# Summing squares over the features: four transposes and a DVE reduction in place of products with a column of ones

## The chip, the cores and the metric

One core of a Trainium2 chip runs the whole program. The metric is device time in microseconds (us) of that core. PE is TensorE (matrix products and transposes), DVE is VectorE, ACT is ScalarE, POOL is GpSimd, SP issues DMAs. PSUM is the memory that TensorE writes into, in banks of 512 fp32 numbers for each of 128 partitions; SBUF is the working memory.

## The reference, cut to what matters

The input x is 16 sequences of 512 tokens with 256 features. For each sequence (a chunk, below):

```python
xn = _layernorm(x, axis=-1)
# branch s, on xn
x1 = causal_dwconv(rmsnorm(xn, conv_norm_g), ...) + xn
x2 = min_gru(rmsnorm(x1, gru_norm_g), gru_w) + x1
s  = gelu(rmsnorm(x2, ff_norm_g) @ w1.T + b1) @ w2.T + b2 + x2
# branch g, on xn
g  = silu(fp4_linear(silu(fp4_linear(xn, w_gate)) * fp4_linear(xn, w_up), w_down))
out = x + s * g
```

with `rmsnorm(x, gamma) = x / max(sqrt(sum(x * x)), 1e-12) * 16 * (gamma + 1)`, the sum over the 256 features. The change is in the second and third rmsnorm, on `x1` and on `x2`. The first is worked out from the layernorm's variance and isn't touched. `fp4_linear` rounds both operands to 4-bit values in blocks of 16; the recurrence of the GRU is a scan along the 512 tokens.

## The kernel before, in words

All weights stay in SBUF. Products of fp32 data are made from two fp32r parts, `_hi` (a copy that ScalarE casts) and `_lo` (what DVE subtracts), as three fp32r products each (`product`, L881). In the s branch the features lie on the partitions and the tokens in the free dimension: `x1`, `xs` and others are 128 x 2 x 512, two blocks `k` of 128 features. DVE adds the two blocks of squares (`add_squares`, L503) into `sqs`, 128 x 512. What is left is the sum over 128 partitions.

Each engine runs its own list of instructions in the written order, and semaphores hold it where it needs another's result. A chunk is `body(c, ...)` on each engine, 16 times: the first without the tail of a chunk before it, the last without the front of one behind it, the 14 between all alike. There the work of three chunks is interleaved by hand: the g branch of chunk c (`gate_up`, `hidden`), the rest of the s and g branches of c - 1 (`hq_transposes`, `down`, `ff2`), and the layernorm, first norm, fp4 rounding and convolution of c + 1 (`front_...`).

A norm goes through these steps, twice in a chunk:

1. ScalarE squares both blocks; DVE `add_squares` (L503).
2. TensorE `sum_squares` (L928): for each of the four tiles of 128 tokens a product of `sqs` with a column of ones, which gives a column of 128 sums, tokens on the partitions.
3. DVE `clamp_sums` (L508) scales by 1/256 and clamps, 128 x 4, into `ss_row`.
4. GpSimd `rms_scale` (L346) raises to the power -1/2, into `inv_rms`.
5. TensorE `spread_scale` (L937) puts the scale of each token on all partitions, by four transposes of a broadcast column.
6. DVE `scaled` (L516) multiplies, ScalarE makes `xs_hi` (L750), DVE `scaled_low` (L522) makes `xs_lo`, and TensorE goes on with `gru` or `ff1`.

For the first norm of a chunk (on `x1`, before `gru`) the sums and the spread scale go to banks 0 and 1 of `w_ps`; for the second (on `x2`, before `ff1`) to two banks of `gu_ps`. On TensorE `gate_up(c, 1, ...)` stands before the first sum and `down(c - 1, 1)` and `gate_up(c, 2, ...)` between it and its spread; `ff2(c - 1, 1)` stands before the second sum and `down(c - 1, 3)` between it and its spread; then `ff2(c - 1, 3)`, `ff2(c - 1, 2)` (L993 is each one's first two transposes) and `ff1`. On DVE the order around the first clamp is

```python
                hidden(c, 1)
                if tail:
                    ratios = fp4_ratios(hid[:, 2, :], NBI, scales)
                ...
                clamp_sums(c * 2, w_ps[:, 0, :])
                if tail:
                    hidden_values(c - 1, 2, fp4_round(NBI, ratios))
                    gelus_low(c - 1, range(5, KF))
                hidden(c, 2)
```

where `hidden` (L475) waits for both products of `gate_up`, and `gelus_low` (L491) makes three low parts. Around the second it is `output(c - 1, 0)` (L549), `clamp_sums`, `front_rows(c + 1)` (L444, the layernorm's rows `xn`, which ScalarE's `xc` at L698 waits for), the scales of the next fp4 rounding, and `scaled`.

Of the kernel before, what the change touches and what calls it, by code (L numbers as in the profile page):

```python
# [23 lines left out]
ALU = mybir.AluOpType  # L24
ACT = mybir.ActivationFunctionType
AX = mybir.AxisListType

P = 128
LN_EPS = 1e-5
NORM_FLOOR_SQ = 1e-24  # L30
# [29 lines left out]
def mixed_recurrent_kernel(nc, x, columns, pw_t, gru_t, w1_t, w2_t, w_gate, w_up, w_down, identity, out):  # L60
    B, L, D = x.shape
    T = L // P
    KD = D // P
# [12 lines left out]
    with ctx:  # L76
        def sb(name, shape, dt=F32):
            return ctx.enter_context(nc.sbuf_tensor(name, shape, dt))
# [10 lines left out]
        def sem(name):  # L89
            return ctx.enter_context(nc.semaphore(name))  # L90


        ident = sb("ident", [P, P])
        ones = sb("ones", [P, P])
        neg_half = sb("neg_half", [P, T])
        carrier = sb("carrier", [P, 1])
        cols = sb("cols", [P, KD * 9 + KF])
# [29 lines left out]
        xq_lo = sb("xq_lo", [P, KD, L], F32R)  # L127

        x1 = sb("x1", [P, KD, L])
        ss_row = sb("ss_row", [P, T])  # L130
        inv_rms = sb("inv_rms", [P, T])
        xs = sb("xs", [P, KD, L])
        sq = xs
        sqs = xs[:, 0, :]
# [104 lines left out]
        dve_step = sem("dve_step")  # L239
# [37 lines left out]
        def over_chunks(engine, body):  # L277

            body(0, 0, False, True)
            for c in range(1, B - 1):  # L280
                body(c, c % 2, True, True)
            return body(B - 1, 1, True, False)


        @block.sync
        def _(sp):
            sp.dma_start(x_in[:], x_v[0]).then_inc(ld_x, 16)
            sp.dma_start(gu_rows[:, 0:NFULL, :],
                         w_gate[0:NFULL * P, :].rearrange("(t p) d -> p t d", p=P)).then_inc(ld_gu, 16)
            sp.dma_start(gu_rows[:, NFULL:2 * NFULL, :],  # L290
                         w_up[0:NFULL * P, :].rearrange("(t p) d -> p t d", p=P)).then_inc(ld_gu, 16)
            sp.dma_start(gu_rows[0:LAST, WT - 1, :], w_gate[NFULL * P:NI, :]).then_inc(ld_gu, 16)
            sp.dma_start(gu_rows[LAST:P, WT - 1, :], w_up[NFULL * P:NI, :]).then_inc(ld_gu, 16)
            sp.dma_start(dn_rows, w_down.rearrange("(t p) n -> p t n", p=P)).then_inc(ld_dn, 16)
            sp.dma_start(w1_f, w1_t.rearrange("(t p) n -> p t n", p=P)).then_inc(ld_w1, 16)
            sp.dma_start(w2_f.rearrange("p a (k n) -> p (a k) n", n=D), w2_t.rearrange("(t p) n -> p t n", p=P)).then_inc(ld_w2, 16)

            def load(c):

                sp.wait_ge(xn_ready, c)  # L300
                sp.dma_start(x_in[:], x_v[c]).then_inc(ld_x, 16)

            def store(c):
                sp.wait_ge(out_ready, c + 1)
                sp.dma_start(out_v[c], o[:]).then_inc(stored, 16)
                sp.dma_start(x_res[:], x_v[c + 1]).then_inc(xres_ready, 16)

            sp.dma_start(x_res[:], x_v[0]).then_inc(xres_ready, 16)
            load(1)
            load(2)  # L310
            with sp.Fori(0, B - 3) as i:
                store(i)
                load(i + 3)
            store(B - 3)
            store(B - 2)
            for t in range(T):
                sp.wait_ge(last_ready, t + 1)
                sp.dma_start(out_v[B - 1][:, t, :], o[:, t, :]).then_inc(stored, 16)
            sp.wait_ge(stored, 16 * (B - 1 + T) + 16)


        @block.gpsimd
        def _(pool):
            steps = Steps(pool_step)
            nc.gpsimd.memset(ones[:], 1.0)
            constants = steps.mark(nc.gpsimd.memset(neg_half[:], -0.5))
            nc.gpsimd.memset(hq[:, :, NI:KI * P], 0.0).then_inc(constants_ready, 1)
            pool.wait_ge(pool_step, constants)

            def layernorm_scales(c, base):  # L330

                steps.start(base)
                pool.wait_ge(stats_ready, c + 1)
                TT = nc.gpsimd.tensor_tensor
                TT(rstd[:], ln_in[:], neg_half[:], ALU.pow).then_inc(rstd_ready, 1)
                pool.wait_ge(rstd_ready, c + 1)
                n = steps.mark(TT(rms_t[:, 1, :], rms_t[:, 0, :], rstd[:], ALU.mult))
                pool.wait_ge(pool_step, n)
                n = steps.mark(TT(rms_t[:, 2, :], rms_t[:, 1, :], rstd[:], ALU.mult))
                pool.wait_ge(pool_step, n)  # L340
                TT(rms0[:], rms_t[:, 2, :], neg_half[:], ALU.pow).then_inc(rms0_ready, 1)

            def rms_scale(n):

                pool.wait_ge(ss_ready, n + 1)
                nc.gpsimd.tensor_tensor(inv_rms[:], ss_row[:], neg_half[:], ALU.pow).then_inc(inv_ready, 1)  # L346

            def output_sum(c, parity):

                pool.wait_ge(sg_ready, T * (c + 1))  # L350
                pool.wait_ge(xres_ready, 16 * (c + 1))
                nc.gpsimd.tensor_tensor(o[:], o[:], x_res[:], ALU.add).then_inc(out_ready, 1)

            layernorm_scales(0, 1)
            for j, (_, src, hi, lo) in enumerate(split_weights):
                for k in range(KD):
                    pool.wait_ge(whi_ready, KD * j + k + 1)
                    nc.gpsimd.tensor_tensor(lo[:, k, :], src[:, k, :], hi[:, k, :].bitcast(F32),
                                            ALU.subtract).then_inc(wlo_ready, 1)

            def body(c, parity, tail, front):
                rms_scale(c * 2)
                if front:
                    layernorm_scales(c + 1, 1 + (c + 1) * 2)
                rms_scale(c * 2 + 1)
                if tail:
                    output_sum(c - 1, 1 - parity)

            over_chunks(pool, body)
# [3 lines left out]
        def _(dve):  # L373
            V = nc.vector
            steps = Steps(dve_step)
# [129 lines left out]
            def clamp_sums(n, bank):  # L505

                dve.wait_ge(ss_done, n + 1)
                V.tensor_scalar(ss_row[:], bank[:, 0:T], 1.0 / D, NORM_FLOOR_SQ / D, ALU.mult,  # L508
                                ALU.max).then_inc(ss_ready, 1)

            def scaled(n, src, bank, ready):
# [26 lines left out]
            def weight_low(p):  # L538
                dve.wait_ge(wqhi_ready, p + 1)
                for (lo, src), (hi, _) in zip(weight_places(p, gu_lo), weight_places(p, gu_hi)):  # L540
                    last = V.tensor_tensor(lo, src, hi.bitcast(F32), ALU.subtract)  # L541
                last.then_inc(wqlo_ready, 1)
# [11 lines left out]
            s = steps.mark(V.tensor_scalar(gains[:], gains[:], 1.0, None, ALU.add))  # L554
            dve.wait_ge(dve_step, s)
            for k in range(KD):
                last = V.tensor_scalar(dww[:, k, :], dww[:, k, :], gains[:, 0, k:k + 1], None, ALU.mult)
# [32 lines left out]

            prologue_steps = steps.n
            quant = 6
            chunk_steps = 4 * quant + 2 * KD + (2 + quant) + KD
            first_steps = chunk_steps - 2

            def body(c, parity, tail, front):
# [15 lines left out]
                else:  # L612
                    down_weight(0)
# [3 lines that stand above are left out]
# [68 lines left out]
        def _(act):  # L685
# [112 lines left out]
            for j, (load, src, _, _) in enumerate(split_weights):  # L798
                act.wait_ge(load, 16)
                if j == 2:  # L800
                    break
                for k in range(KD):
                    A.activation(src[:, k, :], src[:, k, :], ACT.Copy,
                                 scale=gains[:, 1 + j, k:k + 1]).then_inc(wscaled, 1)
            for j, (_, src, hi, _) in enumerate(split_weights):
                for k in range(KD):
                    if j < 2:
                        act.wait_ge(wscaled, KD * j + k + 1)
                    A.copy(hi[:, k, :], src[:, k, :]).then_inc(whi_ready, 1)
# [61 lines left out]
        def _(pe):  # L871
            M = nc.tensor
# [50 lines left out]
            def sum_squares(n, bank, free):  # L923

                pe.wait_ge(sqs_ready, n + 1)
                pe.wait_ge(*free)
                for t in range(T):
                    last = M.matmul(bank[:, t:t + 1], sqs[:, t * P:(t + 1) * P], ones[:, 0:1],  # L928
                                    start=True, stop=True)
                last.then_inc(ss_done, 1)  # L930

            def spread_scale(n, bank, free):
# [74 lines left out]
            for p in range(NFULL + 1):  # L1007
# [4 lines left out]
                for k in range(KD):  # L1012
                    for t in range(tiles):
                        at = (2 * k + t) * P
                        last = M.transpose(w_ps[:, 2 + p % 2, at:at + P],
                                           hq[:, p % 2, t * D + k * P:t * D + (k + 1) * P], ident[:])
# [118 lines left out]
```

## Time and profile before

| | |
|---|---|
| median of 3 runs | 1121.58 us (1121.17 to 1121.89) |
| profiled execution, its own time | 1123.78 us |
| its span, first to last instruction | 1121.9 us |
| mean granted TensorE clock | 0.974 of full |
| busy: PE, PE weight loads, DVE, ACT, POOL | 1057.3, 961.4, 932.6, 603.7, 147.8 us |
| instructions on PE, on DVE | 6818, 1702 |

Times of instructions are from the profiled execution, in us from the start of its span. Matmuls are pipelined, so the busy times of neighbours overlap: how long a group of them holds TensorE is read from the distance between the start of its first and the start of what follows. "Idle before" is the time in which the engine had nothing to run, with the instruction that ended the wait.

### The profile page before, as it was taken

To read this page: it belongs to the slowest core of one execution; us is meant where nothing else is said; L and a number is where in the kernel's file an instruction comes from. 1 tells how busy PE (TensorE), PEld (TensorE's weight loads), DVE (VectorE), ACT (ScalarE), POOL (GpSimd) and SP (SyncE) were. 2 spreads that over 40 slices of the span, in tenths; PEclk is the share of its full clock that TensorE was granted. 3 is DMA by queue.
4 is the path that set the end of the run, shared out by engine and by line. 5 is a ranking of instruction groups with operands and counts; after the bars stand their busy time and mean duration, and the time that the engine had idled before them with its cause. 6 is when DMAs were issued, how large, how long until landed. Compare 5 with 4: busy or idle time off the path is not lost.

```text
span 1121.9 us, 17994 instructions
## 1 busy us (share of the span) xinstructions
PE 1057.3 (94%) x6818; PEld 961.4 (86%) x6818; DVE 932.6 (83%) x1702; ACT 603.7 (54%) x953; POOL 147.8 (13%) x124
## 2 busy tenths in 40 slices
PE   3276999999999999999999999999999999999987
PEld 2174898989989898999989899998989899898977
DVE  5957788998979889888988888888889989798855
ACT  4134556474655737465564746456564746557451
POOL 3101010110201011020202011020101102010010
PEclk9586999999999999999999999999999999999999
DMA  7000001010110101010010101001010100101010
GB/s 239 0 1 19 1 1 57 1 57 1 25 34 1 57 1 58 1 57 1 1 57 1 57 1 58 1 1 57 1 57 1 57 1 23 36 1 39 1 38 20
DMA packets 29364, 31.43 MB, mean 28 GB/s; under 512 B 1120, under 2 KB 28512, under 8 KB 29280
## 3 DMA queue, kind: packets, MB, share of 16 engines
q1 hardware_dynamic: 28448, 29.43, 8.5%
q8 instruction: 55, 0.90, 0.3%
q10 hardware_dynamic: 832, 0.87, 0.2%
q14 instruction: 29, 0.24, 0.1%
HBM read 21.90 MB, written 8.39 MB: 27 GB/s over the span
## 4 chain that ended last, share of the span: by engine, by line
PE 91%; DVE 6%; ACT 2%; issue 1%; DMA 0%; POOL 0%; ACTq 0%; DVEq 0%; POOLq 0%
PE gu_ps L881 46%; PE w_ps L881 32%; PE w_ps L945 4%; PE gu_ps L928 1%; PE w_ps L888 1%; PE w_ps L993 1%; PE w_ps L899 1%; PE gu_ps L888 1%; PE w_ps L928 1%; DVE q_y L398 1%; DVE q_amax L386 1%; PE w_ps L937 1%; PE gu_ps L937 1%; DVE hq L412 1%; DVE q_e L406 0%
## 5 line engine op out<-in xcount | busy, mean ns | idle before, releaser
L881 PE MATMUL gu_ps<-gu_hi,xq_hi 128*128 128x352 f32 x512 | 169.1, 330 | 1.0 <-DVE gu_lo L541 1.0
L881 PE MATMUL gu_ps<-gu_lo,xq_hi 128*128 128x352 f32 x512 | 166.9, 326 | 0.0
L881 PE MATMUL gu_ps<-gu_hi,xq_lo 128*128 128x352 f32 x512 | 166.6, 325 | 0.0
L881 PE MATMUL w_ps<-w_hi,act_hi 128*128 128x256 f32 x480 | 139.6, 291 | 0.0
L881 PE MATMUL w_ps<-w_hi,act_lo 128*128 128x256 f32 x480 | 134.6, 280 | 0.0
L881 PE MATMUL w_ps<-w_lo,act_hi 128*128 128x256 f32 x480 | 134.6, 280 | 0.0
L475 DVE TENSOR_TENSOR hid<-sl,gu_ps 128x704 f32<-128x704 f32 x64 | 56.8, 887 | 83.3 <-PE gu_ps L881 82.8
L881 PE MATMUL w_ps<-dn_hi,hqt_hi 128*128 128x256 f32 x384 | 116.5, 304 | 0.0
L768 ACT ACTIVATE g<-w_ps 128x256 f32<-128x256 f32 x64 | 24.6, 385 | 170.0 <-PE w_ps L881 169.9
L346 POOL TENSOR_TENSOR inv_rms<-ss_row,neg_half 128x4 f32<-128x4 f32 x32 | 40.7, 1270 | 550.2 <-DVE ss_row L508 550.2
L881 PE MATMUL w_ps<-dn_lo,hqt_hi 128*128 128x256 f32 x384 | 108.1, 281 | 0.0
L881 PE MATMUL w_ps<-dn_hi,hqt_lo 128*128 128x256 f32 x384 | 108.1, 281 | 0.0
L881 PE MATMUL gu_ps<-xs_hi,w_hi 128*128 128x512 f32 x256 | 103.6, 405 | 3.1 <-DVE xs_lo L522 3.1
L881 PE MATMUL gu_ps<-xs_hi,w_lo 128*128 128x512 f32 x256 | 102.1, 399 | 0.0
L881 PE MATMUL gu_ps<-xs_lo,w_hi 128*128 128x512 f32 x256 | 101.6, 397 | 0.0
L881 PEld LDWEIGHTS gu_ps<-gu_hi,xq_hi 128*128 128x128 f32 x512 | 97.3, 190 | 1.4 <-DVE gu_lo L541 1.4
L881 PEld LDWEIGHTS gu_ps<-gu_lo,xq_hi 128*128 128x128 f32 x512 | 97.4, 190 | 0.0
L881 PEld LDWEIGHTS gu_ps<-gu_hi,xq_lo 128*128 128x128 f32 x512 | 97.0, 189 | 0.0
L791 ACT ACTIVATE act<-gu_ps,cols 128x512 f32<-128x512 f32 x128 | 86.2, 687 | 15.2 <-PE gu_ps L881 14.8
L881 PEld LDWEIGHTS w_ps<-w_lo,act_hi 128*128 128x128 f32 x480 | 90.6, 189 | 0.0
L881 PEld LDWEIGHTS w_ps<-w_hi,act_hi 128*128 128x128 f32 x480 | 90.5, 188 | 0.0
L881 PEld LDWEIGHTS w_ps<-w_hi,act_lo 128*128 128x128 f32 x480 | 90.4, 188 | 0.0
(127 smaller groups left out, 2635.2 us busy)
## 6 DMA issues: line engine op xcount, KB each, us to landing
x_in<-x_dram SPq DMA_DIRECT2D x16, 512.0 KB, 5.9
x_res<-x_dram SPq DMA_DIRECT2D x16, 512.0 KB, 5.2
out_dram<-o SPq DMA_DIRECT2D x15, 512.0 KB, 3.4
act<-w_t_dram SPq DMA_DIRECT2D x1, 1024.0 KB, 11.8
w_f<-w_t_dram SPq DMA_DIRECT2D x1, 1024.0 KB, 14.3
act<-w_down_dram SPq DMA_DIRECT2D x1, 704.0 KB, 9.8
hid<-w_gate_dram SPq DMA_DIRECT2D x1, 640.0 KB, 6.3
hid<-w_up_dram SPq DMA_DIRECT2D x1, 640.0 KB, 9.3
```

What stands on the lines that cost most here:

```text
L346: nc.gpsimd.tensor_tensor(inv_rms[:], ss_row[:], neg_half[:], ALU.pow).then_inc(inv_ready, 1)
L386: s = steps.mark(V.tensor_reduce(am, blocks(src, nb), AX.X, ALU.max, apply_absolute_value=True))
L398: return steps.mark(V.scalar_tensor_tensor(blocks(q_y[:, 0:nb * FP4_BLOCK], nb), blocks(src, nb), UNIT, spread(q_inv[:, 0:nb], nb), ALU.mu ...
L412: return V.scalar_tensor_tensor(blocks(dst, nb), blocks(q_m[:, 0:nb * FP4_BLOCK].bitcast(BF16), nb), 1.0 / UNIT, spread(q_scale[:, 0:nb], ...
L475: V.tensor_tensor(hid[:, t, :].rearrange("p (h n) -> p h n", h=2), sl[:], gu_ps[:, 1, :, 0:HALF], ALU.mult).then_inc(hid_ready, 1)
L768: A.activation(g[:, t, :], bank[:, 0:D], ACT.Silu).then_inc(g_ready, 1)
L791: A.activation(act1[:, j, :], ff1_bank(j), ACT.Gelu, bias=b1c[:, j:j + 1]).then_inc(gelu_ready, 1)
L881: done = M.matmul(psum, l, r, start=first and i == 0, stop=last and i == len(terms) - 1)
L888: last = M.transpose(bank[:, t * P:(t + 1) * P], src[:, t, k * P:(k + 1) * P], ident[:])
L928: last = M.matmul(bank[:, t:t + 1], sqs[:, t * P:(t + 1) * P], ones[:, 0:1], start=True, stop=True)
L937: last = M.transpose(bank[:, t * P:(t + 1) * P], inv_rms[:, t:t + 1].to_broadcast([P, P]), ident[:])
L945: last = M.transpose(w_ps[:, 2 + k // 4, k % 4 * P:(k % 4 + 1) * P], hq[:, t % 2, k * P:(k + 1) * P], ident[:])
```

## The change

The product with a column of ones becomes a transpose of each 128 x 128 tile of `sqs`, four to a sum, into a whole bank of 128 x 512. Tokens are then on the partitions and the 128 features in the free dimension, and DVE sums those with a TENSOR_REDUCE from PSUM into `ss_sum`, 128 x 4. The clamp reads `ss_sum` after a wait for it. `ones` and its memset go.

```diff
-        ones = sb("ones", [P, P])
...
+        ss_sum = sb("ss_sum", [P, T])
...
-            nc.gpsimd.memset(ones[:], 1.0)
...
                 dve.wait_ge(ss_done, n + 1)
-                V.tensor_scalar(ss_row[:], bank[:, 0:T], 1.0 / D, NORM_FLOOR_SQ / D, ALU.mult,
+                s = steps.mark(V.tensor_reduce(ss_sum[:], bank.rearrange("p (t f) -> p t f", f=P), AX.X, ALU.add))
+                dve.wait_ge(dve_step, s)
+                V.tensor_scalar(ss_row[:], ss_sum[:], 1.0 / D, NORM_FLOOR_SQ / D, ALU.mult,
                                 ALU.max).then_inc(ss_ready, 1)
...
-            chunk_steps = 4 * quant + 2 * KD + (2 + quant) + KD
+            chunk_steps = 4 * quant + 2 * KD + (2 + quant) + KD + 2
...
                 for t in range(T):
-                    last = M.matmul(bank[:, t:t + 1], sqs[:, t * P:(t + 1) * P], ones[:, 0:1],
-                                    start=True, stop=True)
+                    last = M.transpose(bank[:, t * P:(t + 1) * P], sqs[:, t * P:(t + 1) * P], ident[:])
                 last.then_inc(ss_done, 1)
```

`steps` counts the instructions of DVE that another of DVE waits for; a chunk now has two more.

## Rows read from the trace of the kernel before

**Rows 1.** Page, parts 1 and 4: busy time and share by engine; the chain that ended last

```profile
PE 1057.3 (94%) x6818; PEld 961.4 (86%) x6818; DVE 932.6 (83%) x1702; ACT 603.7 (54%) x953; POOL 147.8 (13%) x124
...
PE 91%; DVE 6%; ACT 2%; issue 1%; DMA 0%; POOL 0%; ACTq 0%; DVEq 0%; POOLq 0%
```

**Rows 2.** By stretch: us; PE, PEld, DVE, ACT, POOL busy (count); PEclk; DMA share; GB/s

```profile
95.00:109.00 14.00, 7.49 (x23) 6.07 (x24) 10.98 (x23) 6.31 (x11) 1.29 (x1) 0.51 0.14 39
...
135.00:1045.00 910.00, 910.00 (x5986) 833.01 (x5985) 787.79 (x1423) 516.14 (x814) 124.97 (x99) 1.00 0.08 25
```

**Rows 3.** Instructions of line 928: ns min/median/max, first and last start in us

```profile
L928 PE MATMUL w_ps<-ones,xs x128: 167/250/251, 65.8 to 1039.2; 128*128 128x1 f32 x128
...
L928 PE MATMUL gu_ps<-ones,xs x128: 166/250/372, 96.8 to 1065.6; 128*128 128x1 f32 x128
```

**Rows 4.** Groups by form, DVE: shapes out<-in, count, busy us, mean ns, idle before

```profile
L386 DVE TENSOR_REDUCE q_amax<-hid 128x44 f32<-128x704 f32 x64 | 56.2, 879 | 0.5
...
L533 DVE TENSOR_TENSOR_SCAN xs<-keep,cand 128x512 f32<-128x512 f32 x32 | 39.2, 1225 | 1.1
...
L516 DVE TENSOR_TENSOR xs<-gu_ps,x 128x512 f32<-128x512 f32 x32 | 19.6, 655 | 1.0 <-PE gu_ps L937 1.0
...
L386 DVE TENSOR_REDUCE q_amax<-hid 128x32 f32<-128x512 f32 x5 | 3.4, 675 | 0.0
```

**Rows 5.** Timeline at A, ninth chunk: start us, us, engine, line, instruction, [idle before]

```profile
586.81 0.95 PE L928 MATMUL w_ps<-ones,xs 128*128 128x1 f32 x8
...
587.62 0.36 PE L881 MATMUL w_ps<-dn_hi,hqt_hi 128*128 128x256 f32 x1
...
588.69 0.15 DVE L508 TENSOR_SCALAR ss_row<-w_ps 128x4 f32<-128x4 f32 x1
```

**Rows 6.** Timeline of TensorE around the transposes of `xc`, same chunk

```profile
628.47 1.04 PE L888 MATMUL w_ps<-ident,xc 128*128 128x128 f32 x8
629.26 0.48 PE L881 MATMUL gu_ps<-xs_hi,w_hi 128*128 128x512 f32 x1
```

**Rows 7.** Timeline before the third `hid`, same chunk

```profile
591.83 0.68 DVE L491 TENSOR_TENSOR act_lo<-act,act_hi 128x512 fp32r<-128x512 f32 x1
...
593.70 0.60 PE L937 MATMUL w_ps<-ident,inv_rms 128*128 128x128 f32 x4
593.97 0.89 DVE L475 TENSOR_TENSOR hid<-sl,gu_ps 128x704 f32<-128x704 f32 x1 [1.46 <-PE gu_ps L881]
```

**Rows 8.** Timeline at B, same chunk

```profile
612.49 0.68 DVE L503 TENSOR_TENSOR xs<-xs 128x512 f32<-128x512 f32 x1
...
613.23 1.05 PE L928 MATMUL gu_ps<-ones,xs 128*128 128x1 f32 x8
...
614.14 0.36 PE L881 MATMUL w_ps<-dn_hi,hqt_hi 128*128 128x256 f32 x1
...
614.32 0.16 DVE L508 TENSOR_SCALAR ss_row<-gu_ps 128x4 f32<-128x4 f32 x1 [0.81 <-PE gu_ps L928]
...
614.56 1.29 POOL L346 TENSOR_TENSOR inv_rms<-ss_row,neg_half 128x4 f32<-128x4 f32 x1 [5.30 <-DVE ss_row L508]
...
616.34 0.60 PE L937 MATMUL gu_ps<-ident,inv_rms 128*128 128x128 f32 x4
```

**Rows 9.** Timeline before `ff2(c - 1, 2)`, same chunk

```profile
618.87 0.38 ACT L768 ACTIVATE g<-w_ps 128x256 f32<-128x256 f32 x1
...
619.81 0.38 PE L993 MATMUL w_ps<-ident,x2b 128*128 128x128 f32 x2
```

**Rows 10.** Timeline of the first chunk: A's spread, then B

```profile
72.46 0.65 PE L937 MATMUL w_ps<-ident,inv_rms 128*128 128x128 f32 x4 [1.73 <-POOL inv_rms L346]
...
96.82 1.86 PE L928 MATMUL gu_ps<-ones,xs 128*128 128x1 f32 x8 [5.71 <-DVE xs L503]
...
98.96 1.29 POOL L346 TENSOR_TENSOR inv_rms<-ss_row,neg_half 128x4 f32<-128x4 f32 x1 [10.07 <-DVE ss_row L508]
...
100.31 1.11 PE L937 MATMUL gu_ps<-ident,inv_rms 128*128 128x128 f32 x4 [1.62 <-POOL inv_rms L346]
```


## The prediction

> **What bounds the kernel now.** I read the busy shares first and then the chain that ended last: TensorE is busy 94% of the span and carries 91% of the chain [rows 1]. The busy time by stretch says where that holds. From 135 to 1045 us TensorE is busy for all 910 us at the full granted clock, while DVE has work for 788 of them [rows 2]. That is 14 of the 16 chunks, one period repeated (the sums of the first norm start at 65.8 in the first chunk and at 1039.2 in the last [rows 3], 64.9 us apart on the mean). So a TensorE instruction taken out there shortens the run, unless TensorE then has to wait, and DVE has some 122 us of idle time, 8.7 us a chunk, for more work where the idle time lies right. From 95 to 109 us the granted clock was 0.51 [rows 2]; this is the first chunk, where the engines wait for each other. The rest of the argument is read from the order of instructions at the two places of a chunk where the squares are summed. I call them A (first norm, bank of `w_ps`) and B (second norm, bank of `gu_ps`).
>
> **TensorE's part.** Each sum is four products in the code and eight records in the trace, since a plain fp32 product is issued twice; 128 records of 250 ns for each of the two banks [rows 3]. They overlap. What counts is the distance of starts: at A the next work starts 587.62 - 586.81 = 0.81 us after the first record [rows 5], at B 614.14 - 613.23 = 0.91 us [rows 8]. A transpose of fp32 is one record. Eight of them, followed by an fp32r product as the sums are, take 629.26 - 628.47 = 0.79 us, thus about 0.11 us each and 0.03 for the last [rows 6]; four then take 3 x 0.11 + 0.03 = 0.36 us. A's block becomes 0.45 us shorter. B's becomes up to 0.55 us shorter, of which about 0.1 is a wait for its input that stays: the sum of the halves ends at 612.49 + 0.68 = 613.17 and the block starts at 613.23 [rows 8], while A's, with nothing to wait for, takes the 0.81. TensorE and DVE are in balance there already. The input of B moves with A's gain, because DVE's work between 594 and 613 us starts with a wait for TensorE (`hid`, 1.46 us idle before it) [rows 7] and has no addition in it. So B starts 0.45 us earlier too.
>
> **DVE's part.** Each sum gets a TENSOR_REDUCE of 128x512 from PSUM, and the clamp behind it reads its result through a wait. No row has this reduction. The nearest are a TENSOR_REDUCE of 512 elements from SBUF, 675 ns, one of 704 elements, 879 ns, a two-operand instruction of 512 elements that reads PSUM, 655 ns, and the scan of 512 elements, 1225 ns [rows 4]. The ends are 0.65 and 1.23 us. I take 0.69, from the row that has the same operation and length, and a little for PSUM. With a wait of 0.04 us between reduction and clamp a sum costs DVE 0.73 us more. (VectorE: DVE Perf Modes of the Trainium skill, section Rules for kernel authors, calls `tensor_reduce` its slowest operation, with no faster mode, and advises to restructure where it is on the hot path. The trace has its reduction of 512 elements at 675 ns, beside 655 for a two-operand instruction of that length, so here it is not the slowest; what the rule would make of the sum is the third case below.)
>
> At A the delay lies beside idle time. Behind the clamp DVE quantises, makes three low parts up to 591.83 + 0.68 = 592.51, and idles until 593.97 [rows 7]. With 0.73 more work it ends at 593.24, and the `hid` that it then waits for can start at 593.97 - 0.45 = 593.52: 0.28 us are left. The scale that TensorE spreads at 593.70 has its clamp at 588.69 [rows 5, 7]; with 0.15 for the clamp, 0.08 for the hand-over and 1.3 for GpSimd's power it is there over 3 us before it is needed, and 0.73 + 0.45 fit in. A's cost is nothing, and would be 0.73 - 0.28 if there were no more idle time.
>
> At B it lies on the path. Times from the moment at which the squares are there (613.17) [rows 8]: now the clamp ends at +1.31, the power runs from +1.39 to +2.68, and the spread starts at +3.17 behind `down`, which TensorE has still to finish; without that queue it could start at +2.74 (hand-over 0.06, as from 98.96 + 1.29 to 100.31 in the first chunk [rows 10]). So 0.43 us are in hand. After the change the first transpose is issued at +0.06, the last ends about 0.66 later at +0.72, the reduction runs from +0.76 to +1.45, the clamp from +1.48 to +1.64, the power from +1.72 to +3.01, and the spread starts at +3.07. TensorE arrives there at about +2.7, so it idles for some 0.4 us, which gives back nearly all that B's shorter block gained; B's net gain is 0.10, less about 0.05 because a block after a wait is a little longer. The gain of a chunk is 0.45 + 0.05 = 0.50 us.
>
> **What is late next.** `ff2(c - 1, 2)` needs the bank that ScalarE's `g` (ends 619.25) reads; TensorE comes to it at 619.81 [rows 9]. TensorE moves 0.50 earlier, `g` only some 0.14, because it stands behind `xn` and thus behind the clamp, which ends at +1.64 - 0.45 instead of +1.31. With a hand-over of 0.1 to 0.15 us this comes out at 0 to 0.1 us of waiting; I take 0.04. All else that waits for B's side (the low parts for `ff1`, the transposes of `hq`) has over a microsecond. So 0.46 us a chunk.
>
> **First chunk and the rest.** Before 110 us DVE sets the pace. The spread at 72.46 waited 1.73 us for the power, and the sum's own records were long over, so the 0.73 at A is a loss in full. At B, at about half the clock, the block takes 1.86 us and four transposes about 1.1, by the spread's row [rows 10]: 0.75 earlier against 0.73 later, nothing. Of the 0.73 about half comes back, since TensorE's following products at half speed are fewer before the clock returns at about 109: +0.4 us. The memset of `ones` on GpSimd lies in a time in which GpSimd waits for the statistics: nothing. The last chunk I take at the rate of the others, and its tail, 50 us after its second norm, as unchanged.
>
> Sum: 15 x 0.46 = 6.9 us less, 0.4 more, 6.5 us less. The profiled execution took 1123.78 us by its own time for a span of 1121.9; the median of the runs is 1121.58, 0.2% below it, and the difference is applied to that: 1115.1 us.
>
> **The rivals.**
> 1. As worked out: A gained, B given back. 1115.1; with the reduction between 0.65 and 0.75 and the wait of `ff2` between 0 and 0.1, 0.34 to 0.54 us a chunk, 1114 to 1117. 70%.
> 2. The reduction takes as long as the one of 704 elements, 0.88. B loses 0.19 more a chunk, A's idle time still covers: 0.27 x 15 = 4.0, less 0.6 in the first chunk, 1118.2. A second tight place of the same size would give the same. For it: both reserves that I count on are under 0.3 us. Against: the row of 512. 10%, half of it within 0.2%.
> 3. Slower: the reduction is slow, as the scan's 1.23 us. B loses 0.54 a chunk and turns into a loss, and at A the 1.27 us overrun the idle time by 0.26, which comes through to B's input: 0.46 - 0.54 - 0.26 = -0.34 a chunk, 5.1 us more in all, 1 more in the first chunk, 1127.7. It decides from about 1.05 us on (0.46 = 0.36 + 0.10). Nothing in the rows of reductions speaks for it. 8%. This is also what the skill's rule on `tensor_reduce` would mean if it held for a reduction out of PSUM.
> 4. The clock. The first chunk moves by 0.7 us, and there TensorE is at half speed whenever it has idled. If the full clock returned one such stretch later than 109 us (7 us at half speed cost 3.5 us of TensorE-bound work), the result were 1118.6. The stretch of [rows 2] speaks for the possibility, not for either side. 8%, over a third of it (3%) within 0.2%.
> 5. The clock in every chunk: transposes in place of products make TensorE look idle, and it falls to half speed for 7 us in each chunk. Then 1115 + 15 x 3.5 = 1167. Against it: eight transposes in a row [rows 6] lie in a stretch at the full clock [rows 2]. 1%. TensorE: Matmul & The Clock Gate of the Trainium skill, Part 4, says that the chip doesn't count transposes as busy; that is this case, and the trace bears it out at no place where transposes stand between products.
> 6. Better: B's wait doesn't arise, because TensorE is further behind than I count. Then both blocks are gained, 0.45 + 0.45, 15 x 0.9 - 0.4 = 13.1, 1108.5. 3%.
> That four transposes should cost as much as the eight records is excluded by [rows 6].
>
> **Numbers.** Forecast 1115.1. The range takes the first case, the second and the fourth: 1112.0 to 1119.0. A measurement of this kernel tells no change from one of less than 0.2%, 2.2 us. Faster by more: 70 + 5 + 5 + 3 = 83%; within: 5 + 3 = 8%; slower: 8 + 1 = 9%.
>
> **What would show it.** In the changed kernel the records of the sums should be 128, not 256, with the next product 0.36 us after the first at A. The reduction's mean should be near 0.69 us. DVE's idle time before `hid` at A should be about 0.3 us instead of 1.46. TensorE should idle some 0.4 us before the spread at B and nowhere else in the middle chunks, but for some hundredths at `ff2(c - 1, 2)`. The busy share of TensorE from 135 to 1040 us should fall from 100% to a little over 99%, and the period by some 0.46 us. The forecast fails if the reduction is longer than 0.95 us, if TensorE waits at a place not named, or if the granted clock has another stretch at half.

## The result, and the profile after

The changed kernel takes 1114.14 us (median of 4, 1112.91 to 1114.43) against 1121.38 us (1121.01 to 1121.89): 7.2 us less, ratio 0.9933 with a 95% interval of [0.9916, 0.995], that is 5.6 to 9.4 us. Forecast were 1115.1 us and 6.5 us less. The two profiled executions lie further apart, 1123.78 and 1114.38 us; why is the subject of the last run below.

The page's busy times and chain (parts 1 and 4), as in [rows 1], and the busy time by stretch, as in [rows 2]; the columns are those of the same groups:

```profile
PE 1044.7 (94%) x6690; PEld 946.1 (85%) x6690; DVE 952.9 (86%) x1734; ACT 603.7 (54%) x953; POOL 146.7 (13%) x123
...
PE 62%; DVE 18%; issue 11%; POOL 7%; ACT 2%; DMA 0%; DVEq 0%; ACTq 0%; POOLq 0%
```

```profile
95.00:109.00 14.00, 6.72 (x19) 4.98 (x20) 11.70 (x24) 6.28 (x11) 1.28 (x1) 0.52 0.12 38
135.00:1035.00 900.00, 896.88 (x5858) 817.70 (x5857) 803.65 (x1450) 515.36 (x813) 123.94 (x99) 1.00 0.08 25
```

TensorE has 128 records fewer and is now idle 3.1 us of 900 in the middle, at the full granted clock; DVE has 803.65 us of work there, 24 more than the 779.68 of the kernel before over the same stretch (its second execution, below); the 28 reductions are 19 of them, and most of the rest is that 900 us now hold 14.07 chunks instead of 13.95. The chain changed its look entirely, from 91% TensorE to 62%, for a change of 0.6% in time. That is what a near balance does: one wait of 0.2 us in a chunk is enough to turn the chain off TensorE onto DVE and GpSimd for the stretch before it. How much it costs has to be read from the idle times.

The groups of DVE by form, as in [rows 4], and the waits from 135 to 1035 us (who waited for whom: us in total, times, longest):

```profile
L507 DVE TENSOR_REDUCE ss_sum<-gu_ps 128x4 f32<-128x512 f32 x16 | 11.1, 692 | 7.9 <-PE gu_ps L929 7.9
L507 DVE TENSOR_REDUCE ss_sum<-w_ps 128x4 f32<-128x512 f32 x16 | 10.9, 684 | 0.0
L509 DVE TENSOR_SCALAR ss_row<-ss_sum 128x4 f32<-128x4 f32 x32 | 5.4, 170 | 1.1
```

```profile
PEld gu_ps L937 <- POOL inv_rms L345: 5.9, 14, 0.4
DVE ss_sum L507 <- PE gu_ps L929: 5.8, 14, 0.4
...
PE gu_ps L937 <- POOL inv_rms L345: 3.1, 14, 0.2
```

The reduction takes 684 and 692 ns. The new wait of TensorE is there in all 14 middle chunks, 3.1 / 14 = 0.22 us each, and it is the only one of TensorE's matmuls in that stretch. (VectorE: DVE Perf Modes of the Trainium skill, section The TRN2 errata, gives a formula for the fp32 addition `tensor_tensor`, with 691 ns for 512 elements. It isn't stated for a reduction, but the two rows lie within 1% of it. The advice of the Trainium skill's same page, section Rules for kernel authors, to restructure a `tensor_reduce` on a hot path, bears here on the one at B alone, which is on the path.)

The timeline of the ninth chunk at A, before the third `hid`, and at B, as in [rows 5, 7, 8]:

```profile
583.04 0.60 PE L929 MATMUL w_ps<-ident,xs 128*128 128x128 f32 x4
583.39 0.36 PE L882 MATMUL w_ps<-dn_hi,hqt_hi 128*128 128x256 f32 x1
...
584.92 0.68 DVE L507 TENSOR_REDUCE ss_sum<-w_ps 128x4 f32<-128x512 f32 x1
...
585.64 0.17 DVE L509 TENSOR_SCALAR ss_row<-ss_sum 128x4 f32<-128x4 f32 x1
```

```profile
589.48 0.60 PE L937 MATMUL w_ps<-ident,inv_rms 128*128 128x128 f32 x4
589.75 0.89 DVE L474 TENSOR_TENSOR hid<-sl,gu_ps 128x704 f32<-128x704 f32 x1 [0.33 <-PE gu_ps L882]
```

```profile
608.27 0.68 DVE L502 TENSOR_TENSOR xs<-xs 128x512 f32<-128x512 f32 x1
...
609.00 0.66 PE L929 MATMUL gu_ps<-ident,xs 128*128 128x128 f32 x4
609.41 0.36 PE L882 MATMUL w_ps<-dn_hi,hqt_hi 128*128 128x256 f32 x1
...
609.70 0.69 DVE L507 TENSOR_REDUCE ss_sum<-gu_ps 128x4 f32<-128x512 f32 x1 [0.41 <-PE gu_ps L929]
...
610.42 0.17 DVE L509 TENSOR_SCALAR ss_row<-ss_sum 128x4 f32<-128x4 f32 x1
...
610.67 1.28 POOL L345 TENSOR_TENSOR inv_rms<-ss_row,neg_half 128x4 f32<-128x4 f32 x1 [5.64 <-DVE ss_row L509]
...
611.51 0.28 PE L882 MATMUL w_ps<-dn_hi,hqt_lo 128*128 128x256 f32 x1
...
612.01 0.65 PE L937 MATMUL gu_ps<-ident,inv_rms 128*128 128x128 f32 x4 [0.22 <-POOL inv_rms L345]
```

At A the next product starts 583.39 - 583.04 = 0.35 us after the block's first, in place of 0.81. DVE's idle time before the third `hid` is 0.33 in place of 1.46. At B the block holds TensorE for 0.41 in place of 0.91, and the spread starts at 612.01, 3.06 us after the squares are there (608.27 + 0.68 = 608.95); before it was 3.17.

The gain of a chunk is read best from the period: the distance of A's start in the third chunk from that in the fifteenth, over 12. From chunk to chunk it is 64.52 to 64.55 us in the kernel before and 63.98 to 63.99 in the change, while whole runs of one kernel scatter by 1 to 5 us. All periods of this study:

| kernel | A starts, 3rd and 15th chunk | period | median time |
|---|---|---|---|
| before | 199.62, 974.01 | 64.53 | 1121.38 |
| before_again | 197.64, 972.04 | 64.53 | 1121.01 (1 run) |
| pad16 (before, tiles moved) | 198.07, 972.07 | 64.50 | 1121.71 (1 run) |
| b_only | 197.54, 970.91 | 64.45 | 1120.47 |
| a_only | 199.28, 968.14 | 64.07 | 1115.96 |
| the change | 199.12, 966.94 | 63.98 | 1114.14 |
| after_pad (change, tiles moved) | 199.62, 969.26 | 64.14 | 1117.08 (1 run) |
| extra_a2 | 197.85, 966.51 | 64.05 | 1113.76 (1 run) |
| extra_a4e | 199.10, 969.73 | 64.22 | 1118.61 (1 run) |
| extra_a4 | 200.11, 972.23 | 64.34 | 1120.60 |
| extra_b2 | 197.80, 970.30 | 64.37 | 1119.14 (1 run) |
| fp32r | 197.27, 961.21 | 63.66 | 1107.07 |
| fp32r_al | 198.24, 962.23 | 63.67 | 1107.34 |
| fp32r_al2 | 198.29, 956.75 | 63.21 | 1103.08 |

The ratios below are to runs of the kernel before that were timed beside the run in question. Their medians were 1122.32 us (for a_only, b_only, fp32r and extra_a4), 1122.51 (fp32r_al) and 1122.18 (fp32r_al2), so they don't come out of the table's 1121.38. Of a kernel with one run only the period is used.

### The profile page after: what moved, and what is told of

Same layout as the page of the kernel before. It is cut to its first block, busy times and chain, and to the rows that moved or that the text cites. A ratio compares the mean times of both kernels' runs of the same rounds, so it can differ in the third digit from the quotient of the medians.

```text
span 1112.5 us, 17769 instructions
## 1 busy us (share of the span) xinstructions
PE 1044.7 (94%) x6690; PEld 946.1 (85%) x6690; DVE 952.9 (86%) x1734; ACT 603.7 (54%) x953; POOL 146.7 (13%) x123
## 4 chain that ended last, share of the span: by engine, by line
PE 62%; DVE 18%; issue 11%; POOL 7%; ACT 2%; DMA 0%; DVEq 0%; ACTq 0%; POOLq 0%
PE gu_ps L882 34%; PE w_ps L882 19%; PE w_ps L945 2%; DVE q_y L397 2%; POOL rms L340 2%; DVE hq L411 2%; DVE stats L423 2%; DVE xs L517 2%; POOL inv_rms L345 2%; DVE q_amax L385 2%; POOL rms_t L338 1%; POOL rstd L334 1%; PE w_ps L889 1%; DVE hid L474 1%; DVE hqt_lo L497 1%
```

## The experiments

My theory is that of the prediction: A's shorter block is gained in full because the reduction lies in DVE's idle time, B's is given back. The first rival is that only the number of records on TensorE counts and DVE's work is free, so that both places are worth the same. The second came up with the traces: that a part of the gain is none of the sum's.

### a_only and b_only: half the change each

```diff
+                src = bank[:, 0:T]
+                if n % 2 == 0:      # b_only: == 1
+                    s = steps.mark(V.tensor_reduce(ss_sum[:], bank.rearrange("p (t f) -> p t f", f=P), AX.X, ALU.add))
+                    dve.wait_ge(dve_step, s)
+                    src = ss_sum[:]
...
+                    if n % 2 == 0:  # b_only: == 1
+                        last = M.transpose(bank[:, t * P:(t + 1) * P], sqs[:, t * P:(t + 1) * P], ident[:])
+                    else:
+                        last = M.matmul(bank[:, t:t + 1], sqs[:, t * P:(t + 1) * P], ones[:, 0:1], start=True, stop=True)
```

> Only the first norm's sum (A) by transposes and a reduction, the second's (B) by products as before. Theory: A's shorter block is gained in full, 0.45 us a chunk, and B keeps its cost: 15 x 0.45 = 6.7 us less, about 0.4 more in the first chunk, so about 6.3 us below the kernel before, ratio 0.994. In the trace A steps forward by 0.45 us a chunk, and TensorE isn't idle before B's spread. Rival: every sum is worth the same, since only the number of TensorE's records counts: half of the change, 3.6 us less, ratio 0.997.

> Only the second norm's sum (B) by transposes and a reduction. Theory: the reduction lies on the path here and gives back all but 0.10 us a chunk: 1.5 us less, ratio 0.9987, with TensorE idle 0.2 to 0.4 us before B's spread in each chunk. Rival: as before, 3.6 us less, ratio 0.997.

Measured: a_only 1115.96 us, 6.4 less than before, ratio 0.9942 [0.9926, 0.9959], period 64.07, 0.46 below before. b_only 1120.47 us, 1.9 less, ratio 0.9982 [0.9973, 0.9992], period 64.45, 0.08 below. Together 0.54 of the change's 0.55 us. Both add a tile, which alone shortens the period by 0.03 (pad16, below); against that kernel's 64.50 they gain 0.43 and 0.05. a_only has no wait of TensorE before a spread in the middle chunks; b_only has the same one as the change, 14 times, 3.1 us:

```profile
PE gu_ps L946 <- POOL inv_rms L347: 3.1, 14, 0.3
```

The two places aren't worth the same, by a factor of more than five, and the first rival is out.

### extra_a4, extra_a4e, extra_a2, extra_b2: more work for DVE

```diff
                 dve.wait_ge(ss_done, n + 1)
+                if n % 2 == 0:      # extra_b2: == 1
+                    V.tensor_reduce(ss_two[:, 0:w], bank[:, 0:w * P].rearrange("p (t f) -> p t f", f=P), AX.X, ALU.add)
                 s = steps.mark(V.tensor_reduce(ss_sum[:], bank.rearrange("p (t f) -> p t f", f=P), AX.X, ALU.add))
```

with w = 4 or 2. In extra_a4 `ss_two` lies beside `ss_row`, in the others behind all tiles.

> The changed kernel with a second reduction of 128x512 at A, whose result nobody reads. Theory: DVE had 0.33 us of idle time left before the third hid; the second reduction takes 0.61 (0.69 less an overlap of 0.08), so 0.28 us a chunk run over and come through to B's input and the period: 4.2 us above the change plus 0.6 in the first chunk, some 2.4 us below the kernel before, ratio 0.998. Rival (DVE has over 5 us of idle time a chunk, so its work costs nothing): as the change, ratio 0.9935.

> The changed kernel with a second reduction at A over half of the bank (256 elements, about 0.41 us, 0.33 of it added), written to a tile behind all others, so that no address moves. Theory: DVE had 0.33 us of idle time left before the third hid, and the extra work fits in just: the period stays at 63.99 to 64.02. Rival (DVE's added time costs in proportion, as the 0.3 us a chunk for 0.6 of the whole extra reduction might suggest): 64.15.

> The changed kernel with the second reduction over the whole bank at A, as before, but written to a tile behind all others, so that no address moves. Theory: DVE's reserve at A is its idle time of 0.33 us and the overlap of 0.08 us that an instruction behind a wait doesn't have, 0.41 us; 0.60 us of work overrun it by 0.19: period 63.99 + 0.19 = 64.18, not the 64.29 with the moved tiles. Rival (the extra 0.30 were all DVE's work): 64.29.

> The changed kernel with a second reduction at B over half of the bank (256 elements, 0.33 us added), written to a tile behind all others. Theory: B's reduction lies on the path to the spread, where TensorE already waits, so all of it comes through: period 63.99 + 0.33 = 64.32, TensorE's idle time before B's spread from 0.22 to 0.55 us. The same addition at A cost 0.01 us. Rival (work for DVE is worth the same in both places): 64.00.

Measured: extra_a4 1120.60 us, ratio 0.9991 [0.9982, 1.0001], period 64.34: 0.36 above the change, more than the 0.28 us a chunk that I expected, and the reason wasn't DVE alone. From A to B it takes 26.17 us on the mean, as extra_a4e does, against 25.97 in the change; the rest of its excess lies between B and the next A, 38.18 against extra_a4e's 38.05, as in after_pad, which has the same addresses (38.14 against the change's 38.02). With the addresses kept, extra_a2's period is 64.00 at the median (63.98 to 64.00 in 12 of 14 chunks, 64.34 and 64.35 in the other two), extra_a4e's 64.17, 0.18 above the change. A half reduction adds 0.33 us of work and costs 0.02; a whole one adds 0.60 (its two reductions start at 585.95 and 586.55) and costs 0.18. So DVE has about 0.41 us to spare at A. In extra_a4e the third `hid` has no idle time before it any more:

```profile
589.15 1.89 DVE L491 TENSOR_TENSOR act_lo<-act,act_hi 128x512 fp32r<-128x512 f32 x3
590.96 0.88 DVE L475 TENSOR_TENSOR hid<-sl,gu_ps 128x704 f32<-128x704 f32 x1
```

The two odd chunks have another reason than the reserve. In each of these traces single instructions of DVE start some 0.35 us later than in the neighbouring chunks. In extra_a2 and extra_a4e they are one that writes `hq` in the tenth chunk (at 14.9 and 15.1 us after A's start in the neighbouring chunks, 0.37 later here) and one of `front_rows` in the fourteenth, late by 0.34 to 0.36. Both stand behind the third `hid`, where the reserve doesn't help, and extra_b2, whose reserve at A is untouched, has such a chunk too (64.67, the fourteenth). In the change the late one is the second `hid` of the fifth chunk: DVE comes to the clamp 2.95 us after A's start instead of 2.60, the third `hid` still starts on time, and the period isn't longer. There the reserve took it up. What makes single instructions late stays open.

At B half a reduction costs 64.35 - 63.98 = 0.37 at the median, 0.33 expected, and TensorE waits that much longer:

```profile
610.52 0.43 DVE L509 TENSOR_REDUCE ss_two<-gu_ps 128x2 f32<-128x256 f32 x1 [0.41 <-PE gu_ps L932]
610.86 0.68 DVE L510 TENSOR_REDUCE ss_sum<-gu_ps 128x4 f32<-128x512 f32 x1
...
613.17 0.65 PE L940 MATMUL gu_ps<-ident,inv_rms 128*128 128x128 f32 x4 [0.56 <-POOL inv_rms L346]
```

At the median the same instruction costs 0.02 us at A and 0.37 at B, which is the theory in one pair of runs.

### fp32r: shorter on TensorE, nothing added on DVE

```diff
-        ones = sb("ones", [P, P])
+        ones = sb("ones", [P, 2])
+        ones_r = sb("ones_r", [P, 2], F32R)
...
-        sqs = xs[:, 0, :]
+        sqs = sb("sqs", [P, L], F32R)
...
-                    last = M.matmul(bank[:, t:t + 1], sqs[:, t * P:(t + 1) * P], ones[:, 0:1],
+                    last = M.matmul(bank[:, 2 * t:2 * t + 2], sqs[:, t * P:(t + 1) * P], ones_r[:],
```

The clamp reads every second column, and DVE fills `ones_r` from `ones` once at the start. The squares' sum is rounded to fp32r, so the arithmetic isn't quite that of the other two kernels.

> The kernel before, with the squares' sum written as fp32r and multiplied with two fp32r columns of ones: one record for each product instead of two, no reduction on DVE. The sum of the squares is rounded to fp32r before it is summed over the features. Theory: both blocks become 0.45 us shorter and nothing is added to the path at B, so 0.9 us a chunk: 13.5 us less than before and some tenths more in the first chunk, ratio 0.987 to 0.988. Rival (only records count, the reduction is free): as the change, 7.2 us less, ratio 0.9935.

Measured: 1107.07 us, ratio 0.9862 [0.9846, 0.9879] where I had expected 0.987 to 0.988, period 63.66, 0.87 below before. B in this kernel:

```profile
605.17 0.59 PE L930 MATMUL gu_ps<-ones_r,sqs 128*128 128x2 f32 x4
...
605.81 0.16 DVE L509 TENSOR_SCALAR ss_row<-gu_ps 128x4 f32<-128x4 f32 x1 [0.36 <-PE gu_ps L930]
...
606.05 1.29 POOL L347 TENSOR_TENSOR inv_rms<-ss_row,neg_half 128x4 f32<-128x4 f32 x1 [4.85 <-DVE ss_row L509]
...
607.85 0.60 PE L939 MATMUL gu_ps<-ident,inv_rms 128*128 128x128 f32 x4
```

The scale is there at 607.34, before TensorE comes to the spread at 607.85, without a wait. The time is that of the prediction's sixth case, 0.9 us a chunk, reached by taking the reduction off the path. It is faster than the change by 0.32 us a chunk.

### pad16, after_pad, fp32r_al, fp32r_al2: where the tiles lie

The products of 512 columns (`gru`, `ff1`) are the same in all kernels, yet in before their starts lie 234.6 ns apart on the mean (851 neighbouring pairs from 200 to 1000 us) and in the change 233.6. One unused tile was put into each kernel where the change has `ss_sum`:

```diff
+        ss_pad = sb("ss_pad", [P, T])
         ss_row = sb("ss_row", [P, T])
```

fp32r_al moves `ones_r` behind all other tiles, fp32r_al2 `ss_row`.

> The kernel before with one unused tile of 128x4 where the changed kernel has its new tile, nothing else. It moves xs, xs_hi, xs_lo and all tiles behind them from an address of 32 modulo 64 bytes to 0. Theory: the fp32r products of 512 columns (gru, ff1), whose starts lie 234.6 ns apart in the kernel before and 233.6 in the change and in both of its halves, are sped up by the address and not by the change: 233.6 here, and a period of 64.46 us instead of 64.53. Rival: the slower DVE traffic of the old sum, or the chip, makes the difference: 234.6, 64.53.

> The changed kernel with the same unused tile, which moves xs_hi, xs_lo and those behind them back to 32 modulo 64. Theory (address): products 234.6 to 235.2 ns apart, period 64.06 to 64.1 instead of 63.99. Rival (not the address): 233.6 and 63.99.

> The version with fp32r products of ones, with the small tile of ones moved behind all others, so that xs_hi and xs_lo lie at 0 modulo 64. The sum of the squares is rounded to fp32r before the features are summed. Theory: period 63.66 - 0.07 = 63.59, 1 us below the fp32r version, about 15.5 us below the kernel before, ratio 0.986. Rival (address without effect): as the fp32r version, 63.66.

> The fp32r version with one tile (ss_row) moved behind all others, so that both the weights gru_hi and w1_hi and the data xs_hi and xs_lo lie at 0 modulo 64; in the last try the weights had moved to 32. The sum of the squares is rounded to fp32r before the features are summed. Theory (both addresses have to be at 0): starts of the products of 512 columns 233.6 ns apart instead of 234.5 and 234.8, period 63.56 to 63.60, 1 to 1.5 us below the fp32r version, ratio 0.985. Rival (it was something else in the layout, not these): 234.5 and 63.66.

Addresses in the compiled program modulo 128, and the mean distance of starts:

| kernel | gru_hi, w1_hi | xs_hi, xs_lo | distance, ns |
|---|---|---|---|
| before, before_again | 64 | 32 | 234.6, 234.7 |
| pad16 | 64 | 64 | 233.65 |
| a_only, b_only | 64 | 64 | 233.65, 233.7 |
| the change, extra_a2, extra_a4e, extra_b2 | 64 | 64 | 233.6 to 233.7 |
| after_pad, extra_a4 | 64 | 96 | 235.1, 235.2 |
| fp32r | 0 | 96 | 234.5 |
| fp32r_al | 96 | 64 | 234.8 |
| fp32r_al2 | 0 | 64 | 230.6 |

So it is the layout: pad16, whose instructions are those of before, has the 233.65, and after_pad, measured on the same chip, 235.1. My first rule, the data's address at a multiple of 64, held for the layouts before it and failed in fp32r_al, where the same edit had pushed the weights off theirs. With both at multiples of 64 the distance was 233.6 or 230.6, so this isn't the whole rule, and which address makes the last 3 ns stays open. Products of 256 columns change too: from fp32r to fp32r_al2, which moves `xs_hi` and all tiles behind it, those of `down` go from 119.4 to 115.0 ns and those of `ff2` from 118.5 to 115.7, while those of `gate_up`, whose weights and data keep their places, stay at 163.0 and 162.9. In time it matters nearly as much as the change itself: fp32r_al2 differs from fp32r by one 16-byte tile's place and takes 1103.08 us (ratio to before 0.9819 [0.9802, 0.9836]), period 63.21 against 63.66, where I had expected 63.56 to 63.60 and a ratio of 0.985. It is the fastest version of this study.

The worth for the change: pad16 0.03 us a chunk below before, after_pad 0.15 above the change. In pad16 the time from A to B is as before (26.41 and 26.42 us), so the gain at `gru` is lost, as it would be if DVE sets the time up to B; only that behind B is left.

### before_again: one kernel, two executions

> The kernel before once more. Theory: the profiled execution of before lay 2.2 us above the median of its runs because of where the granted clock returned in the first 110 us. The period is 64.53 again, and what differs between the two executions, up to 2.5 us, lies ahead of the second chunk and in the tail, with the clock's stretches at half speed placed otherwise. Rival: the middle chunks differ too.

Measured: 1121.01 us, span 1119.2 against 1121.9; period 64.53 in both. A's start in the second chunk is at 133.09 instead of 135.08, so 2.0 of the 2.7 us lie ahead of it; 0.7 lie behind B of the last chunk. The granted clock's stretches differ: here it was at half from 28 to 59 us (0.50), in the first execution (the first line below) until 61.3,

```profile
24.00:61.00 37.00, 14.11 (x49) 10.40 (x48) 27.90 (x62) 10.07 (x22) 8.69 (x4) 0.59 0.00 0
...
28.00:59.00 31.00, 10.29 (x36) 7.89 (x37) 25.35 (x58) 6.21 (x16) 4.37 (x2) 0.50 0.00 0
59.00:79.00 20.00, 15.98 (x106) 15.40 (x105) 12.86 (x23) 4.13 (x6) 1.01 (x1) 1.00 0.00 1
```

and the lead of the second execution grows where its clock is back at full and the first one's is still at half: counted in the first one's time, from 0.3 us at 59 to 1.3 at 62, from 1.3 at 87 to 1.9 at 89, from 1.5 at 108 to 2.0 at 115, and from 2.0 at 1090 to 2.7 at 1096. In the changed kernel's trace the clock was at half from 31 to 58 and again from 72 to 75, and in its tail for 3 us, where the first execution of before had 7 (0.54 from 1089 to 1096):

```profile
1082.00:1085.00 3.00, 2.84 (x14) 2.87 (x15) 2.93 (x7) 0.38 (x1) 0.00 (x0) 0.50 0.00 0
```

So two executions of one kernel can lie 2.7 us apart, more than the 2.2 us by which the profiled executions' 9.4 exceed the medians' 7.2. Differences of one or two microseconds outside the middle chunks are not to be read as the change's.

## Why the prediction was right

Point by point, by its own steps:

- **TensorE's part.** A's block 0.35 us for the predicted 0.36, B's 0.41 with its wait of 0.05. Right.
- **DVE's part.** The reduction 0.684 and 0.692 us for 0.69. The case in which it is slow (third) and that of 0.88 (second) fell with it. The price came from the row with the same operation and length; the reading from PSUM added 0.01 to 0.02. The wait of 0.04 us between reduction and clamp had no row behind it; it measured 0.04 at A (584.92 + 0.68 to 585.64) and 0.03 at B.
- **A.** DVE's idle time left 0.33 us for 0.28, and a_only gains 0.46 us a chunk for 0.45, 0.43 of it without the tiles' part. extra_a2 and extra_a4e bear the reserve out from both sides: one nearly uses it up, the other overruns it.
- **B.** The spread starts +3.06 after the squares for +3.07. The profile gives the idle time as 0.22, from the modelled end of the last product, which overlaps the next start by 0.16 when there is no wait; from start to start (611.51 to 612.01) the gap is 0.50 in place of 0.12, thus 0.38 for my 0.4. b_only gains 0.08 us a chunk, 0.05 of it without the tiles' part, for my 0.05.
- **What is late next.** `ff2(c - 1, 2)` doesn't wait; the 0.04 us were not there, and they didn't follow from my own numbers. The 0.56 us between the end of `g` and the start of `ff2` shrink by 0.50 and grow by 0.14, which leaves 0.20, more than the hand-over of 0.15 that I allowed. It is 0.21, from 614.97 + 0.39 = 615.36 to 615.57:

```profile
614.97 0.39 ACT L769 ACTIVATE g<-w_ps 128x256 f32<-128x256 f32 x1
...
615.57 0.38 PE L993 MATMUL w_ps<-ident,x2b 128*128 128x128 f32 x2
```

- **First chunk.** From A to the spread 6.64 us before, 7.37 after (64.15 to 71.52), 0.73 more; from B to the spread 3.49 and 3.47. Both as worked out. How much of the 0.73 comes back is read from after_pad, whose clock changed its level at the same times as in the first execution of before, within 0.2 us: from A to the second chunk's A it takes 69.71 us for 69.27, thus 0.44 more for my 0.4.
- **The clock in the first chunk.** One of my signs of being wrong did appear, another stretch at half. TensorE waits 2.91 us before A's spread instead of 1.73 [rows 10], and at the end of that wait the granted clock fell, to half from 71.7 to 75.1 us:

```profile
71.52 0.79 PE L937 MATMUL w_ps<-ident,inv_rms 128*128 128x128 f32 x3 [2.91 <-POOL inv_rms L345]
```

```profile
58.00:72.00 14.00, 11.09 (x70) 10.79 (x70) 8.04 (x14) 3.44 (x5) 1.01 (x1) 0.99 0.00 1
72.00:75.00 3.00, 3.00 (x14) 3.00 (x13) 0.33 (x1) 0.80 (x1) 0.00 (x0) 0.50 0.00 0
```

Of the 14 traces seven have the reduction at A, and there the wait is 2.91 to 3.51 us; six of them have this stretch, from within 1.4 us of the wait's end, all but after_pad. None of the other seven has it, with waits of 1.73 to 2.17 us. So the change makes it likely, and it isn't certain. Whether the longer wait brings it or the transposes do, no run separates. The change takes 70.98 us from A to the second A, 1.3 more than after_pad, though its other stretches differ too. The fourth case had the right kind of loss in another place. Its premise, that TensorE is at half speed there whenever it has idled, is too strong: from 89 to 96 us TensorE was busy for 2.20 of 7 us in the change's trace, at 0.97.
- **The sum.** 0.55 us a chunk for 0.46: 0.04 is the wait of `ff2` that isn't, 0.03 the tiles' addresses, which the prediction didn't have and pad16 shows, and 0.02 the rest. That is 15 x 0.55 = 8.2 us; less the 0.44 of after_pad's first chunk 7.8, less another 1.3 with the extra stretch 6.5; measured are 7.2, in an interval of 5.6 to 9.4. The mechanism held, but that the total came within 1 us of the forecast is in part luck: 1.3 us more in the chunks and up to 1.3 lost to the clock stand against each other.
- **The clock in every chunk** (fifth case): 1.00 from 135 to 1035 us. (TensorE: Matmul & The Clock Gate of the Trainium skill, Part 4, says that transposes don't count as busy in the way products do; the middle chunks show no effect of it.)

## What to carry to other kernels

Before a piece of work is moved from the busy engine to another, look at what that engine does around each place where it would land: the same reduction was free behind one sum, where DVE idled 1.5 us before its next wait, and took back over four fifths of the gain behind the other, where the next engine waited for it. A price is best taken from a row with the same operation and length, and a reserve is best tested by work that just fits and work that just doesn't. When a kernel is timed after an edit that adds or drops a tile, compare also an unchanged group of instructions in both traces, since the layout alone can be worth nearly as much as the edit.

## What the runs showed of the hardware that was not expected

- The distance of starts of equal fp32r products of 512 columns depends on where weights and data lie in SBUF: 230.6 to 235.2 ns over six layouts, and 0.46 us in a period of 63.66 by one tile's place (fp32r against fp32r_al2). Which addresses are good ones is not settled.
- An fp32r product with two columns holds TensorE as long as a transpose of 128: four in 0.36 us at A. Eight records with one column took 0.81. So up to 128 columns the number of records set the price of such small products, some 0.11 us each, and not their columns.
- One kernel's granted clock falls and returns at other times from execution to execution in the first 110 us and in the tail, 2.7 us of span between two executions with the same middle.
- A longer wait of TensorE in the first chunk (2.9 us and more instead of 2.2 and less) went with a stretch of 3.4 us at half the clock at its end in six of seven traces, against none of seven.
